# Moving the state-space block into the other instruction stream, with the scan cut in two and PSUM banks assigned by use

## The reference, cut to what matters

```
xn = layernorm(x)
s  = selective scan of xn (forward 16 states, backward 16 states), + D*xn     # "scan": 32 state steps
g  = silu(mixture-of-experts gelu FFN of xn)                                  # "prologue" has this and the scan's inputs
x1 = x + s*g
xn = layernorm(x1)
q  = rope(xn W); h = rmsnorm(q)                                               # "head"
s  = out_proj(rmsnorm((ssd(conv(h W)) + D*..) * silu(z))) + q                 # state-space block, "mamba"
for l in 0, 1:                                                                # "layers", on shifted tokens
    xn = xn + local_attention(xn) wo ; xn = xn + gated gelu FFN(layernorm(xn))
out = x1 + s * silu(xn)
```

## Time and profile before

| | |
|---|---|
| median of 3 runs | 4470.81 us (4470.54 to 4471.91) |
| the profiled execution, its time and its span | 4473.03 us, span 4471.2 us |
| busy share of PE / DVE / ACT / POOL | 77% / 56% / 56% / 38% |
| mean granted TensorE clock | 0.923 of full speed |

### The profile page before, as it was taken

The page is one execution under the profiler, slowest core; times in us unless marked ns, Lnnn a source line. Parts: engine busy times, 40 slices in busy tenths (PEclk is TensorE's granted clock), DMA queues, the critical chain, the costliest instruction groups (busy, mean ns, idle before and its releaser), DMA issues. The chain is left out here.

```text
span 4471.2 us, 55299 instructions
## 1 busy us (share of the span) xinstructions
PE 3462.7 (77%) x16160; PEld 1873.6 (42%) x16160; DVE 2481.5 (56%) x4239; ACT 2513.2 (56%) x5798; POOL 1718.4 (38%) x1428
## 2 busy tenths in 40 slices
PE   5787778877878788787777778778787787878776
PEld 1344344444444444344443444434444444444443
DVE  6565654646556465564655646565464655646433
ACT  4455556555656555555654555556565555655554
POOL 2253442524425254252533425344252442525332
PEclk9798998989999899998999989999998999989998
DMA  1000000000000000000000000000000000000000
GB/s 77 3 1 1 5 1 5 1 1 6 1 6 1 1 5 1 6 1 6 1 1 6 1 6 1 1 6 1 6 1 1 6 1 6 1 1 3 1 3 3
DMA packets 18390, 20.53 MB, mean 5 GB/s; under 512 B 768, under 2 KB 17152, under 8 KB 17792
## 3 DMA queue, kind: packets, MB, share of 16 engines
q1 hardware_dynamic: 18048, 16.44, 1.1%
HBM read 12.24 MB, written 4.19 MB: 4 GB/s over the span
## 5 line engine op out<-in xcount | busy, mean ns | idle before, releaser
L1393 POOL TENSOR_TENSOR hc<-hst,Cs 128x512 f32<-128x512 f32 x512 | 649.4, 1268 | 1721.2 <-DVE hst L1165 1696.1
L1165 DVE TENSOR_TENSOR_SCAN hst<-dA,bank 128x512 f32<-128x512 f32 x512 | 625.0, 1221 | 337.0 <-ACT dA L862 150.3
L518 PE MATMUL bank<-W,xs 128*128 128x512 f32 x960 | 474.6, 620 | 128.8 <-DVE tmp L1305 126.8
L494 PE MATMUL bank<-hc,C 128*128 128x512 f32 x1024 | 553.9, 624 | 0.8 <-POOL hc L1393 0.7
L506 PE MATMUL bank<-parts,sel 96*128 96x512 bf16 x1024 | 363.4, 410 | 219.1 <-DVE hst L1165 193.5
L1157 DVE TENSOR_TENSOR bank<-u,bank 128x512 f32<-128x512 f32 x512 | 351.9, 687 | 322.7 <-PE bank L506 293.0
L868 ACT COPY Cs<-bank 128x512 f32<-128x512 f32 x512 | 298.5, 583 | 351.8 <-PE bank L506 351.2
L1454 POOL TENSOR_TENSOR oT<-tmp 128x512 f32<-128x512 f32 x256 | 324.3, 1267 | 329.8 <-PE bank L670 168.9
L993 ACT ACTIVATE Pm<-bank,mx 128x128 f32<-128x128 f32 x1024 | 362.3, 369 | 118.0 <-DVE mx L1325 118.0
L1469 POOL TENSOR_TENSOR Pm<-Pm,rinv 128x512 f32<-128x512 f32 x256 | 266.0, 1039 | 376.4 <-DVE rinv L1318 358.9
L862 ACT ACTIVATE dA<-delta,neg_a 128x512 f32<-128x512 f32 x512 | 371.3, 725 | 4.9 <-issue 4.1
(11 more groups left out here) (221 smaller groups left out, 6085.2 us busy)
## 6 DMA issues: line engine op xcount, KB each, us to landing
W<-wpack SPq DMA_DIRECT2D x1, 4498.0 KB, 13.6
x_tok<-x SPq DMA_DIRECT2D x16, 256.0 KB, 3.6
out<-xa SPq DMA_DIRECT2D x16, 256.0 KB, 3.5
rot<-tables SPq DMA_DIRECT2D x2, 512.0 KB, 16.2
wc_f<-taps SPq DMA_DIRECT2D x1, 1024.0 KB, 19.5
C<-cpack SPq DMA_DIRECT2D x1, 721.0 KB, 14.8
Pm<-mask SPq DMA_DIRECT2D x1, 320.0 KB, 15.1
tmp<-rowpack SPq DMA_DIRECT2D x1, 256.0 KB, 17.4
```

The source lines that it names most:

```text
L494: mm(y_acc[:, :], ident, hc[:, k % 2, :], start=(k == 0), stop=(k == 2 * NS - 1))\
L518: mm(b[:, :], weights, rhs, start=True, stop=True).then_inc(full(ring, job), 1)
L1165: v.tensor_tensor_scan(o, a, b, 0.0, ALU.mult, ALU.add).then_inc(sem("a_h"), 1)
L1393: g_.tensor_tensor(hc[:, k % 2, :], hst[:, k % 2, :], Cs[:, k % 2, :], ALU.mult)\
```

## The change

The state-space block leaves stream B and becomes stage `mamba(i)` of stream A, behind `head(i)`; its jobs move from ring B to ring A. Its temporaries move from stream B's tiles (kT, oT, vt, Pm, on) to tiles of stream A that the scan has just finished with (hst, hc, bx, delta, u, dA, Cs, gate, dlow). The scan is divided: steps 0 to 11 of the next batch stand at the end of stream A's round (behind `prologue(i+1)`), steps 12 to 31 at its start. Stream B is now only the two layers and what ends the batch. Banks of ring A are chosen by `home`: B_k has bank k % 2 of the ring, C_k the third, every other job the least recently used.

```
-        def run(e, prologue, scan, head, stage_b, finish):
+        def run(e, prologue, scan, head, mamba, stage_b, finish):
-            alone(chain(prologue(0), scan(0), head(0), prologue(1)))
-            both(chain(scan(1), head(1), prologue(2)), stage_b(0, None))
+            def ready(i):
+                return chain(prologue(i), scan(i, 0, CUT)) if CUT else prologue(i)
+            def body(i):
+                return chain(scan(i, CUT, 2 * NS), head(i), mamba(i))
+            alone(chain(ready(0), body(0), ready(1)))
+            both(chain(body(1), ready(2)), stage_b(0, None))
...
-            both(chain(scan(NB - 1), head(NB - 1)), stage_b(NB - 2, NB - 3))
+            both(body(NB - 1), stage_b(NB - 2, NB - 3))
             alone(stage_b(NB - 1, NB - 2))
...
-LAYER = 11
+LAYER = 1
-PACE = [(0, 2), (LAYER, 16), (LAYER + UNITS_END, 28), (LAYER + LAYER_SLOTS, HEAD), (LAYER + LAYER_SLOTS + 5, PRO),
-        (LAYER + LAYER_SLOTS + UNITS_END, A_SLOTS - 1), (B_END, A_SLOTS - 1), (B_SLOTS, A_SLOTS)]
+PACE = [(0, 0), (LAYER, 2), (LAYER + UNITS_END, HEAD + 5), (LAYER + LAYER_SLOTS, MAMBA + 5),
+        (LAYER + LAYER_SLOTS + 7, PRO), (LAYER + LAYER_SLOTS + UNITS_END, SCAN1), (B_SLOTS, A_SLOTS)]
...
+SCAN_HOME = {f"{name}{k}": k % 2 if name == "B" else 2 for name in "BC" for k in range(2 * NS)}
+def home(jobs, n):
+    at, order = [], list(range(n))
+    for name, _, _ in jobs:
+        b = SCAN_HOME.get(name, order[0])
+        order.remove(b)
+        order.append(b)
+        at.append(b)
+    return at
...
-        big1 = kT[:, :, :].rearrange("p q (h l) -> p q h l", h=HM)
-        big2 = oT[:, :, :].rearrange("p q (h l) -> p q h l", h=HM)
-        xbc, sz, y3 = vt[:, 0:4], vt[:, 4:6], PT
+        heads_of = [t.rearrange("p (h l) -> p h l", h=HM) for t in
+                    (hst[:, 0, :], hst[:, 1, :], hc[:, 0, :], bx[:, 0, :], bx[:, 1, :], hc[:, 1, :], gate[:, :])]
+        big1, big2 = [None] + heads_of[0:3], heads_of[3:7]
+        xbc = [delta[:, 0, :], delta[:, 1, :], u[:, 0, :], u[:, 1, :]]
+        sz, ysq, y_r, sm1 = dA, u, xc, sm
...
             def stage_b(i, ended):
+                yield 0
+                shifted(xs0, xn2, "t_xs", "m_xn", i, 1)
...
                 f(tmp2[:, 0, :], yB[:, :], ACT.Silu).then_inc(sem("g2"), 1)
+                tables()
```

More of the change, by code:

```diff
@@ L264, in build @@
         sm = sb("sm", [T])
+        smb = sb("smb", [T])
         tmp1 = sb("tmp1", [2, T])
@@ L495, in accumulate @@
                         .then_inc(sem("a_yacc"), 1)
[L497 to L500, removed]
+                yield scan_slot(lo)
+                if lo == 0:
+                    pe.wait_ge(*step("a_parts", i))
+                for k in range(lo, hi):
+                    yield scan_slot(k)
                     d, s = k // NS, k % NS
@@ L722, in stage_b @@
                         n = s - UNIT
+                        if l == 0 and s == 2 and ended is not None:
+                            finish(ended)
                         if s < NT:
@@ L771, in finish @@
                 last.then_inc(sem("xo_full"), 1)
-            run(pe, prologue, scan, head, stage_b, finish)
+            run(pe, prologue, scan, head, mamba, stage_b, finish)
         @block.scalar
@@ L824, in prologue @@
                 yield PRO + 4
+                if later(i):
+                    act.wait_ge(*before("m_sm1", i))
                 for d in range(2):
@@ L853, in prologue, with scan @@
                 tables()
-            def scan(i):
-                yield SCAN
-                act.wait_ge(*step("a_delta", i))
-                for k in range(2 * NS):
-                    yield SCAN + k
+            def scan(i, lo, hi):
+                yield scan_slot(lo)
+                if lo == 0:
+                    act.wait_ge(*step("a_delta", i))
+                for k in range(lo, hi):
+                    yield scan_slot(k)
                     if k >= 2:
@@ L949, in stage_b @@
                         n = s - UNIT
+                        if l == 0 and s == 3:
+                            if ended is not None:
+                                finish(ended)
+                            act.wait_ge(*step("a_x1", i))
+                            nc.scalar.copy(x1b[:, :], x1[:, :]).then_inc(sem("m_x1b"), 1)
                         if s < NT:
@@ L1030, in finish @@
                 nc.scalar.copy(xo[:, :], o_acc[:, :]).then_inc(sem("xo"), 1)
-            run(act, prologue, scan, head, stage_b, finish)
+            run(act, prologue, scan, head, mamba, stage_b, finish)
         @block.vector
@@ L1285, in stage_b @@
                     yield at_l
-                    if l == 0:
-                        dve.wait_ge(*step("m_sm", i))
+                    if l == 0 and later(i):
+                        dve.wait_ge(*before("x2", i))
                     for s in range(UNITS_END):
@@ L1361, in finish @@
                 pass
-            run(dve, prologue, scan, head, stage_b, finish)
+            run(dve, prologue, scan, head, mamba, stage_b, finish)
         @block.gpsimd
@@ L1380, in prologue, with scan @@
                     .then_inc(sem("a_parts"), 1)
-                prior.append(step("a_parts", i))
-            def scan(i):
-                prior.clear()
-                for k in range(2 * NS):
-                    yield SCAN + k
+                pool.wait_ge(*step("a_parts", i))
+            def scan(i, lo, hi):
+                if lo == CUT:
+                    prior.clear()
+                for k in range(lo, hi):
+                    yield scan_slot(k)
                     pool.wait_ge(*step("a_h", i, k + 1))
@@ L1473, in finish @@
                 pass
-            run(pool, prologue, scan, head, stage_b, finish)
+            run(pool, prologue, scan, head, mamba, stage_b, finish)
 SETUP = 7 + 4 + 3 + 2 + TAPS + 1 + 2 + len(TABLES) * NL
```

313 lines of the change are left out of this document (162 added, 151 removed).

## The result

The changed kernel takes 4617.3 us (4596.28 to 4625.22, 4 runs) against 4471.4 of before: ratio 1.0313, interval 1.0271 to 1.0354. It is **3.1% slower**, where 4258 (range 4060 to 4450) was forecast. The profiled execution took 4625.22 us, the longest of the four.

A forecast was written before the change was run, and what follows sets the result against it. No engine was full (PE busy 77%), so a chain through several engines was taken as the limit. Four stretches summed to 258.0 us a round; 388.8 + 15 rounds gave 4258 us, range 4060 to 4450.

The forecast's parts named there:

- Layer 0: Stream B's slots 1 to 15, with 18 scan steps and the head's first five slots: 73.2 to become 93.7 us.
- the price of six more scan steps at 1.64 us: In layer 0, from twelve steps of before: +9.8 us; bounds for a step 1.47 and 1.86 us.
- The head, 12 us: Head's slots 0 to 4 on layer 0's last three slots: +12 us, bounds 8.4 and 20.
- FFN of layer 0: Slots 16 to 20, losing 4 steps, gaining the head's end and block's first groups: +6 on 22.0, 28.0 us.
- Layer 1: Slots 21 to 35, prologue kept, rest of the block added: +20.5 (bounds +13.5 and +37), 96.0 us.
- rival C: Slower: block's chain laid bare in layer 1, stopping both streams; up to 287.5 us a round and 4701; chance 0.14.
- Layer 1's FFN and the turn: Slots 36 to 42 and 0, with 14 steps, eight in a row taking 14.9 us: 28.9 to become 40.3 us.
- The ends: Start gains block and 12 steps, end loses the block, last round loses 30.5: 388.8 us plus 15 rounds.
- The banks: Bank change removes L543's wait for the scan, 193.5 us in all, to under 40; credited 1.3 in layer 0.
- Table loads: On ACT, from 10 to 12 a round, +2.6 us, hidden in layer 1's FFN and costed at nothing.
- Rival B: Streams interleave almost perfectly, fewer gaps lift the clock; round under 246 us, for instance 240 and 3990; chance 0.09.
- PE at 0.85 or more busy in the last stretch: Sign the forecast is right: PE this busy from wo of layer 1 to the next projections.

The follow-up runs named there:

- the best kernel: Changed kernel with head and block later, 13 of layer 0's 18 scan steps in its first twelve slots, 5 in the last three: 4380.17 us, ratio 0.9792.
- banks by use: Kernel before with ring A's banks alone changed (B_k in banks 0 and 1 in turn, C_k always in bank 3): 4429.99 us, ratio 0.9907.
- the kernel with CUT = 8: Changed kernel with head and block later, with 8 scan steps instead of 12 at a round's end, 22 in layer 0: 4446.84 us, ratio 0.9934.

## Why the prediction was wrong

**Layer 0, 107.4 for 93.7.** The step that failed is the price of six more scan steps at 1.64 us. Forecast without the head was 73.2 + 9.8 − 1.3 = 81.7. With steps spread evenly the measured value is 84.3, so the price was nearly right (1.71 for 1.64, and no credit for the bank). That was in part luck: the layer's 73.2 us in the earlier trace rows is that of two rounds of the fourteen, the others take 69.8 to 71.6 and typically 70.4, from which a step is 1.41 us, and against 70.4 the six added steps cost 2.3 us each even when spread. But the changed PACE runs through 24 slots of stream A in 15 of the layer's, so the 18 steps end three slots early, and that alone makes 92.0: +10.3 against the forecast. I had written in the same paragraph that the head falls on the last three slots, and still took a price measured on twelve steps spread over fifteen. Its upper bound was wrong too: 1.86, the pace of the scan alone, is no bound where a step stands in another stream's latency chain; packed steps cost 2.14 on average and the last three of the middle part 2.6 each.

**The head, 12 us.** Measured 11.2 (103.2 for 92.0). Right, but the FFN got back 8.3 of it.

**The clock.** What is left of layer 0 is 4.2 us. The changed kernel's last round and its typical one run the same list in layer 0 at two clocks; the typical row stands above, the last is:

```profile
4217.50:4320.70 103.20, 76.11 (x389) 42.04 (x392) 62.28 (x97) 59.55 (x155) 53.52 (x46) 0.92 0.01 3
```

At 0.92 PE is busy 76.11 us of 103.2, at 0.85 81.05 of 107.4: of 4.9 us more of PE's time 4.2 show in the stretch. Sum: 10.3 − 0.8 + 4.2 = 13.7.

**FFN of layer 0, 35.3 for 28.0.** The block's first five slots were bounded by 4.7 and 11 with +6 taken. They cost the whole 11.4 (35.3 − 23.9). The head's end, which came at nothing, costs 1.9 (23.9 − 22.0). PE's own new work in these slots is 12.5 us (30.02 above, 17.54 in the same FFN with the block later), where I had counted 11, and almost none of it went into the 6.3 us that PE idles there alone: 5.3 are idle still.

**Layer 1, 96.9 for 96.0.** Right. The block's convolution, states and output add 21.4 to the prologue's 20.5, and the waits of rival C stay small there: PE's longest at the block's lines is 4.6 us, for ACT at the convolution. With the whole block in it (the best kernel) the layer is 109.8, 34.3 us for the block, where the block alone has PE busy 36.2.

**Layer 1's FFN and the turn, 43.7 for 40.3.** Eight scans at 1.86 behind the down projection were to take 14.9 us. DVE's scans do start 1.84 to 1.93 apart within a group, but starts 4.12 and 5.08 apart lie between the groups, where DVE does stream B's end of batch and ACT the copies into xs. From L801's end (3346.5) to the next projections (3366.9) it is 20.4 us, 5.5 more. The six steps ahead of it, and the copies, were over-priced by 2.1 in return.

**The ends.** Mean round 283.0, first 255.5 us, last round 242.5, stream B's end 163.3: together 4623.3. The last round is 40.5 shorter than the others for the 30.5 forecast, mostly because its last stretch, without the twelve steps, is shorter by 18.3 and not by 11. The sum's form was right to 10 us.

**The banks.** A wait in L543's row went from 193.5 for one engine to 190.1 for another, and the edit is nevertheless worth 41 us before and 265 us after. I had credited 1.3 in layer 0, and told nothing else of it. In the old order the wait itself fell by 130 us for these 41.

**Table loads.** Two more a round at 1283 ns, as forecast (193 in all for 164): L891, the gate's, is one of them, with 0.3 us idle ahead of all its sixteen. The Trainium skill, page ScalarE: Activation LUTs, section What ACT_TABLE_LOAD costs, adds a drain of about 1380 ns to each. No row here shows it: beside the short idle time ahead, ACT's next instruction, where it is ready, starts within 0.02 us of a load's end.

**The rivals.** The sign was that of rival C, given 0.14, and its place was wrong: not the block in layer 1, but the scan's and the head's chains in layer 0. That its price of 287.5 a round was near the 283.0 is luck. Rival B fell: the mean clock is 0.898, below the 0.923 of before, and 0.67, between the clock's two levels of 1.2 and 2.4 GHz, in the head's 21 us at the end of layer 0, where PE is busy 14.10 of 21.20. Its reading of the clock was also too simple: in the earlier trace rows the block at 0.98 has PE no busier (0.80 of the stretch) than layer 0 at 0.91 (0.82). PE at 0.85 or more busy in the last stretch didn't come either: 33.68 of 43.70 is 0.77.

Where the 15 us a round went: in the best order the block's 64.0 us go, and layer 0 takes 10.7 more than the 73.2 of the earlier trace rows, its FFN 6.8, layer 1 25.9, and the last stretch 13.8, 57.2 in all. The gain of 6.8 us is under half of what I forecast, and banks by use gave 3 of it without any move.

## What to carry to other kernels

A price per step read from spread steps holds only for spread steps: it stayed at 1.7 us from 0.9 to 1.5 steps a slot as long as steps went on to the layer's last slots, and was 2.14 where they ended early. When a table of slots is changed, count the steps per slot first, above all in the slots that get none, and take the price for each part of the stretch. In this kernel the bulk had to reach to the last slots of the other stream's chain, and a second chain (the head) set on those slots cost 11 us and gave back 8. A wait that changes its releaser and keeps its sum has not stayed the same wait: what it waits for can be nearer or farther, and only a run with that one edit tells its worth. Before a large move is dropped because it is slower, its pacing is worth a few runs: here it was 5.1% of the time (4617.3 to 4380.2).

## What the runs showed of the hardware

The same stretch of the same program ran in some rounds at one mean clock and in others at another, inside one execution (0.89 and 0.96 below, 0.85 and 0.92 above). Layer 0 of the kernel with CUT = 8 in two of its rounds:

```profile
2676.00:2773.40 97.40, 78.50 (x391) 43.42 (x390) 63.74 (x97) 60.52 (x157) 56.03 (x47) 0.89 0.02 6
3219.10:3310.40 91.30, 72.15 (x391) 38.81 (x390) 63.08 (x97) 60.27 (x157) 56.04 (x47) 0.96 0.02 7
```

PE has the same 391 records and is busy 6.4 us longer; the stretch is 6.1 us longer, while DVE, ACT and POOL do theirs in the same time to within 1.1%. PE's time is passed on almost in full although PE is idle 19 us of each; that it is a link of the stretch's chain would explain it, and was not traced. So a round's length was uncertain by 4 to 6 us for the clock alone, and a forecast made from one round should look at the clock of several. What decides between the two was not tried.
